# Recurrence of a gated delta rule: q/k/v projections from fp32 to three fp32r passes, turns in another order

## What is computed

```python
q = einsum('btd,cd->bct', h, Wq)      # k and v likewise; h is (4, 1024, 256), C = 1024
q = silu(causal_conv(q))              # depthwise, four taps, bias; k and v likewise
k = k / norm(k)
a, b = sigmoid(h Wa + ba), sigmoid(h Wb + bb)
S = clip(a*S + b*outer(v - a*(S k), k), -5, 5)     # per token, batch and head
y = S q
y = y * silu(h Wg + bg);  out = y Wo
```

## Time and profile before

| | us |
|---|---|
| runs of the kernel | 1858.39, 1866.88, 1870.13 |
| median | 1866.88 |
| span of the profiled execution | 1869.6 |
| that execution's own time | not listed apart; the nearest listed run is 0.5 above the span |
| front, to the first `turn_matrix` | 0 to 55.5 |
| turns (first to last `clear_x`) | 57.5 to 1109.6 |
| last chain, with gate products | 1170 to 1247 |
| `attn_out` | 1247 to 1510 |
| `moe` | 1510 to 1870 |

### The profile page before, as it was taken

How to read it: one execution, slowest core, us unless ns; L and a number is a source line. 1 busy time by engine, 2 the same in 40 slices (tenths; PEclk the granted TensorE clock), 3 DMA queues, 4 the chain that set the end, 5 groups by cost and what they waited for, 6 DMA issues and landing times. The chain is left out here.

```text
span 1869.6 us, 59680 instructions
## 1 busy us (share of the span) xinstructions
PE 1620.9 (87%) x24736; PEld 1142.6 (61%) x24736; DVE 1389.8 (74%) x1892; ACT 895.2 (48%) x1768; POOL 1127.0 (60%) x1362
## 2 busy tenths in 40 slices
PE   7778999999988989999988988835999848999997
PEld 4445666666666656566656666625888836666664
DVE  8777888888898888898898887447787664444443
ACT  5745555555655655655556555313444232222221
POOL 0657768768767767768777768017343103666664
PEclk9989989989999999989999988977999859999998
DMA  5221231231231231231231230246333163455543
GB/s 184 49 53 25 69 91 37 67 93 37 67 92 37 67 93 36 67 93 36 69 92 36 65 75 26 69 144 227 135 128 110 46 230 79 94 93 100 96 91 51
DMA packets 89465, 156.59 MB, mean 84 GB/s; under 512 B 15708, under 2 KB 54116, under 8 KB 88108
## 3 DMA queue, kind: packets, MB, share of 16 engines
q1 hardware_dynamic: 73292, 124.80, 22.6%
q0 software_dynamic: 15904, 27.93, 8.1%
HBM read 112.56 MB, written 40.12 MB: 82 GB/s over the span
## 5 line engine op out<-in xcount | busy, mean ns | idle before, releaser
L1386 PE MATMUL d_ps<-hT,turn_shared 128*128 128x512 f32 x768 | 402.8, 632 | 8.4 <-DVE d_Vp L1171 4.6
L953 POOL TENSOR_TENSOR turn_shared<-turn_shared,d_tmp 128x31 f32<-128x31 f32 (+15 forms) x496 | 289.7, 584 | 38.9
L948 POOL TENSOR_TENSOR d_tmp<-turn_shared 128x31 f32<-128x31 f32 (+15 forms) x496 | 286.4, 577 | 38.9
L1024 DVE SCALAR_TENSOR_TENSOR turn_shared<-d_ps,d_cw,turn_shared 128x1023 f32<-128x1023 f32 (+2 forms) x192 | 245.3, 1278 | 15.0 <-ACT turn_shared L682 12.6
L742 ACT ACTIVATE d_S<-d_S,gamma_chunk 128x64 f32<-128x64 f32 x448 | 130.9, 340 | 184.5 <-DVE d_S L1052 144.6
L2539 POOL DMA_INDIRECT m_xt<-rows_scratch,m_slot_i x71 | 70.2, 989 | 183.3 <-DVE m_slot_i L2632 95.7
L1386 PEld LDWEIGHTS d_ps<-hT,turn_shared 128*128 128x128 f32 x768 | 126.8, 192 | 87.6 <-issue 71.4
L2526 ACT ACTIVATE m_hm<-m_ps,m_b_tile 128x128 f32<-128x128 f32 x284 | 80.9, 368 | 206.3 <-PE m_ps L2706 206.3
L122 PE MATMUL o_po<-wo_split,y_high 128*128 128x256 f32 x512 | 101.7, 302 | 44.8 <-DVE y_low L115 44.8
L2549 POOL DMA_INDIRECT out<-m_yo,m_slot_i x71 | 114.2, 1608 | 41.2 <-issue 20.3
L2696 PE MATMUL m_ps<-m_w,m_xs 128*128 x284 | 136.2, 602 | 1.6 <-DVE m_xs L2641 1.0
(11 more groups left out here) (251 smaller groups left out, 3737.2 us busy)
## 6 DMA issues: line engine op xcount, KB each, us to landing
turn_shared<-steps_scratch SPq DMA_DIRECT2D x64, 256.0 KB, 4.2
d_qg<-gamma_scratch SPq DMA_DIRECT2D x64, 256.0 KB, 5.0
y_scratch<-d_yT SPq DMA_DIRECT2D x256, 64.0 KB, 1.8
d_arow<-ab_scratch SPq DMA_DIRECT2D x128, 128.0 KB, 3.1
y<-y_scratch SPq DMA_DIRECT2D x8, 2048.0 KB, 8.7
m_w<-w_in SPq DMA_DIRECT2D x16, 512.0 KB, 10.0
turn_shared<-x_by_half_in SPq DMA_DIRECT2D x8, 512.0 KB, 6.8
rows_scratch<-gates SPq DMA_DIRECT2D x4, 1024.0 KB, 11.6
```

Source lines behind the costliest of these rows:

```text
L948: nc.gpsimd.tensor_tensor(tv, Tq[:, s + 1:, s].rearrange("p (r a) -> p r a", a=1).broadcast_to([P, left, known]), X[:, s, 0:known].rearran ...
L953: nc.gpsimd.tensor_tensor(X[:, s + 1:, 0:known], X[:, s + 1:, 0:known], tv, ALU.subtract).then_inc(s_sub, 1)
L1024: nc.vector.scalar_tensor_tensor(out=dst[:, j + 1:], in0=src[:, 0:T - 1 - j], scalar=cw[:, u // BP % 2, n, 2 - j:3 - j], in1=dst[:, j + 1: ...
L1386: return nc.tensor.matmul(dst[:, g, :], w[:, m % 2, n, dc, :], hT[:, dc, at:at + G], start=(dc == 0), stop=(dc == DC - 1))
```

## The change

It does four things.

1. **Projections.** `proj` calls `three`: each of the 24 products of a turn becomes three fp32r passes over high and low parts of the weights and of the input. The parts of the input are made in the front: ACT writes the high part (`high_part`, one 128x1024 instruction for each of the eight pieces), POOL the low part (`low_part`, a subtraction of 128x1024). The parts of the weights are made for every turn and each of q, k, v: ACT `high_weights` and POOL `low_weights`, 128x256 each. The low part takes the place of the raw weights, and there is one buffer, so a load must wait for the projections of the turn before.
2. **Order of turns.** u now runs over the blocks first: turns 0 to 7 are batches 0 and 1, turns 8 to 15 batches 2 and 3.
3. **One pair on chip.** High and low parts of two batches take the room of `hT`. The parts of batches 2 and 3 go to DRAM from a staging buffer in the front (`store_input`), those of batches 0 and 1 after it (`store_pair`, 4 MB). Turn 7 loads batches 2 and 3 (`load_pair`, 2 MB each), turn 15 batch 0 again for the gate; `load_gate_input` and `load_h` fetch the parts for the other gate products.
4. **Splits of the input leave DVE**: `split_input` and `split_h` are gone, and the gate reads its moving operand in pieces of 32 tokens out of the stored parts.

The core of the diff (SP, ACT and POOL issue orders shortened to the new calls with their neighbours; the order on PE is the same, and on DVE only the splits go):

```diff
+    def high_part(act, g):
+        act.wait_ge(s_e, g + 1)
+        if g >= GH * BP + 2:
+            act.wait_ge(s_hst[g % 2], 32 * ((g - GH * BP) // 2))
+        nc.scalar.activation(part_of(0, g).bitcast(F32R), h_full[:, g % 2], ACT.Identity).then_inc(s_hh, 1)
+    def low_part(pool, g):
+        pool.wait_ge(s_hh, g + 1)
...
+        nc.gpsimd.tensor_tensor(part_of(1, g).bitcast(F32R), h_full[:, g % 2], part_of(0, g),
+                                ALU.subtract).then_inc(s_hl, 1)
+    def store_input(sp, g):
+        sp.wait_ge(s_hl, g + 1)
+        for a in range(2):
+            sp.dma_start(h_d[a, :, :, g * G:(g + 1) * G], h_sp[:, g % 2, a]).then_inc(s_hst[g % 2], 16)
     def alphas(act):
         act.wait_ge(s_a, B * GH)
+        for k in range(2):
+            act.wait_ge(s_hst[k], 16 * GH * BP)
@@ SP @@
-            def weights(m): ...
+            def weights(u, n):
+                if u and n == 1:
+                    sp.wait_ge(s_kproj, 2 * u)
+                elif u:
+                    sp.wait_ge(s_qproj, 4 * u - 2 + n)
+                sp.dma_start(w_raw[:, n], wqkv[block_of(u)][:, n]).then_inc(s_w[n], 16)
             step_rows(0, 0)
+            f.store_input(sp, 4)
             step_rows(0, 1)
+            f.store_input(sp, 5)
+            weights(1, 1)
+            f.store_input(sp, 6)
+            f.store_input(sp, 7)
...
             f.store_alphas(sp)
+            weights(1, 2)
             step_rows(1, 1)
             step_rows(2, 0)
+            store_pair()
             for it in range(1, TURNS + 2):
+                if new_k:
+                    weights(un, 1)
+                    conv_weights(un)
                 if prep:
                     gamma_rows(u)
                 if bound:
                     store_y(tb, 1)
+                if new_k:
+                    weights(un, 0)
+                if it in (M - 1, TURNS - 1):
+                    load_pair(it, 0, BP if it == M - 1 else 0)
+                if it == M - 1:
+                    load_pair(it, 1, BP + 1)
+                if new_k:
+                    weights(un, 2)
@@ ACT, front @@
             f.keep(act, 0)
+            f.high_part(act, 0)
             f.root(act, 1)
             f.keep(act, 1)
+            f.high_part(act, 1)
             f.logits(act, 0)
+            high_weights(0, 1)
...
+            f.keep(act, 4)
+            f.high_part(act, 4)
             first_k(0, 0)
-            f.keep(act, 4)
+            f.logits(act, 4)
             f.keep(act, 5)
+            f.high_part(act, 5)
+            high_weights(0, 0)
+            f.logits(act, 5)
             f.keep(act, 6)
+            f.high_part(act, 6)
             first_k(0, 1)
+            f.logits(act, 6)
             f.keep(act, 7)
+            f.high_part(act, 7)
             silu_k(0, 0)
...
             first_v(0, 1)
             f.alphas(act)
+            high_weights(1, 2)
             silu_v(0, 1)
             first_k(1, 0)
@@ ACT, loop: high_weights(un, 1) in slot 0, (un, 0) in slot 4, (un, 2) in slot 9 @@
@@ POOL, loop @@
                 if prep:
                     clear_x(u)
-                    solve(u)
+                    solve(u, range(8))
+                if new_k:
+                    low_weights(un, 1)
+                if prep:
+                    solve(u, range(8, CH - 1))
...
                     decay_k(u, 1)
+                if new_k:
+                    low_weights(un, 0)
+                    low_weights(un, 2)
@@ PE @@
             def proj(dst, n, b2, u, i):
-                m, g, dc = u // BP, i // DC, i % DC
-                at = (2 * (u % BP) + b2) * T + g * G
-                return nc.tensor.matmul(dst[:, g, :], w[:, m % 2, n, dc, :], hT[:, dc, at:at + G],
-                                        start=(dc == 0), stop=(dc == DC - 1))
+                g, dc = i // DC, i % DC
+                at = b2 * T + g * G
+                return three(nc, dst[:, g, :], lambda a: w_sp[a][:, n, dc, :], lambda a: h_in[:, a, dc, at:at + G],
+                             dc == 0, dc == DC - 1)
```

More of the change, by code:

```diff
@@ L452, with __init__, __call__, first @@
 AT_KT, AT_VT, AT_Z = (0, 0), (1, 1), (1, 1)
+class Early:
+    def __init__(self, nc, stack):
+        self.nc, self.stack = nc, stack
+    def __call__(self, name, *shape):
+        return self.stack.enter_context(self.nc.sbuf_tensor(name, list(shape), F32))
+    def first(self, name, *shape):
+        with ExitStack() as for_now:
+            return for_now.enter_context(self.nc.sbuf_tensor(name, list(shape), F32))
 def delta_fast(nc, sem, x, cT, wmod, rw, ident_d, ones2_d, wab, bab, tri_d, ident, ones2, modT, rw_sb, gates_s, s_loaded,
[L456 removed]
+               wqkv, convp, mask_d, h_in, h_d, w_raw, w_sp, btT, gtok, dec, gC, ab_s, a0_s, g_s, y_s, fmax, flag, wg, bg, turn,
+               gate1, held, split, bg_sb, s_gate):
     s_gw, s_hi, s_ws, s_hs, s_gp, s_g = s_gate
[L458 removed]
+    s_c, s_ar = sem("d_const"), sem("d_alpha_rows")
+    s_w = [sem(f"d_weights_{n}") for n in "qkv"]
+    s_wh, s_wl = [sem(f"d_weights_high_{n}") for n in "qkv"], [sem(f"d_weights_low_{n}") for n in "qkv"]
+    s_cw = [sem("d_conv_even"), sem("d_conv_odd")]
+    s_pair, s_pst = [sem(f"d_h_pair_{b2}") for b2 in range(2)], sem("d_h_stored")
     s_kproj, s_kfirst, s_ksilu = sem("d_k_proj"), sem("d_k_first"), sem("d_k_silu")
@@ L635, in _ @@
             f.load(sp, 0)
-            weights(0)
+            conv_weights(0)
+            for n in (1, 0, 2):
+                weights(0, n)
             f.load(sp, 1)
@@ L670, in _ @@
                     alpha_rows(tc, 0)
-                if prep and u % BP == BP - 1 and u // BP + 2 < M:
-                    weights(u // BP + 2)
                 if it == TURNS - 1:
@@ L841, in _ @@
             first_q(0, 1)
+            high_weights(1, 1)
             first_v(0, 0)
@@ L873, in _ @@
                         keep_w(tc, 1)
+                    if new_k and c == 0:
+                        high_weights(un, 1)
                     if prep and c == 1:
@@ L892, in _ @@
                         carry_state(tc, 5)
+                    if new_k and c == 4:
+                        high_weights(un, 0)
                     if prep and c == 5:
@@ L909, in _ @@
                         carry_state(tc, 10)
+                    if new_k and c == 9:
+                        high_weights(un, 2)
                     if new_k and c == 10:
@@ L953, in substitute, with low_weights, solve @@
                 nc.gpsimd.tensor_tensor(X[:, s + 1:, 0:known], X[:, s + 1:, 0:known], tv, ALU.subtract).then_inc(s_sub, 1)
-            def solve(u):
-                scale_rows(u)
-                for row in range(CH - 1):
+            def low_weights(u, n):
+                pool.wait_ge(s_wh[n], u + 1)
+                nc.gpsimd.tensor_tensor(w_sp[1][:, n].bitcast(F32R), w_raw[:, n], w_sp[0][:, n],
+                                        ALU.subtract).then_inc(s_wl[n], 1)
+            def solve(u, rows):
+                for row in rows:
+                    if row == 0:
+                        scale_rows(u)
                     substitute(u, row)
@@ L993, in decay_k @@
                                         ALU.mult).then_inc(s_kd, 1)
+            for g in range(2):
+                f.low_part(pool, g)
+            low_weights(0, 1)
+            for g in range(2, 6):
+                f.low_part(pool, g)
+            low_weights(0, 0)
+            for g in range(6, B * GH):
+                f.low_part(pool, g)
+            low_weights(0, 2)
             clear_x(0)
-            solve(0)
+            solve(0, range(10))
+            low_weights(1, 1)
+            solve(0, range(10, CH - 1))
+            low_weights(1, 0)
             gamma_k(0)
@@ L999, in _ @@
             decay_k(0, 1)
+            low_weights(1, 2)
             for it in range(1, TURNS + 2):
@@ L1985, in _ @@
             nc.vector.memset(raw[:, 0:4], 0.0).then_inc(s_z, 1)
+            dve.wait_ge(s_h, 32)
+            for dc in range(DC):
+                nc.vector.tensor_tensor(hT[:, dc, :], hT[:, dc, :], h_low[:, dc, :], ALU.add).then_inc(s_hj, 1)
             with dve.Fori(0, M) as m:
@@ L2216, in load_x, with load_h @@
                 sp.dma_start(held(g), x[:, g * GT:(g + 1) * GT, :]).then_inc(s_loaded[g % XHOLD], 16)
+            def load_h(b):
+                for a in range(2):
+                    sp.dma_start(h_s[b % 2][:, a], h_d[a, :, :, b * T:(b + 1) * T]).then_inc(s_hs, 16)
             load_y(0)
```

246 lines of the change are left out of this document (147 added, 99 removed).

## The result

The changed kernel takes 1893.2 us (median of 4 runs, 1887.8 to 1900.1), the kernel before 1867.9 in the same session: a ratio of 1.0143, 95% interval 1.0111 to 1.0175. That is slower by more than the 1% that a measurement tells, and 1.2 us above the range of 1856 to 1892. The profiled execution took 1896.0, its span is 1894.4; against the profiled 1869.6 it is 24.8 us longer, and that is the sum to be explained.

The account below looks back on a forecast made before the run. The prediction took a turn's loop, with POOL's triangular solution setting its floor, as the bound. Terms 8.0 - 1.3 + 4.5 + 0.5 - 4 - 2.2 - 1.0 = +4.5 us gave 1871 us, range 1856 to 1892.

Parts of the forecast that it names:

- So POOL sets a floor ..., and the whole excess over it is 1.4 us: Turns 1 to 14: POOL's solution and the shortest tail give 68.7 us under a turn of 70.06.
- Heads: 14 x 0: From `clear_x` to `rows_of_x` in fourteen turns: cheaper products and added POOL work leave the mean at 45.6; no change.
- Products: Projections on PE: three fp32r passes take 0.96 us for 1.12, saving 3.8 us of PE a turn.
- Rival 4: Projections: passes cost as much as fp32, savings vanish and heads grow; +20 us, 1887; chance 0.04.
- POOL in the head: `low_weights(un, 1)` after row 7 of `solve` adds 0.73 us, raising the head's floor to 45.6.
- Tails: From `rows_of_x` to the next `clear_x`: cheaper products save 0.3 us a turn, -4 over fourteen.
- Front: Start to first `turn_matrix`: ACT's added splits and a store wait move it from 55.5 to 63.5, +8.0 (+3 to +13).
- The wait of `high_part(7)`: In the front, ACT waits for `store_input(5)` to land, starting at 52 where it could at 50.3; +1.7 us.
- The wait behind `alphas`: Turn 0: `high_weights(1, 2)` waits 4.8 us for its weights, delaying `first_k(1, 0)`; +4.5 us, bounds 3 and 6.
- Stores and loads of the pair: 4 MB of stores ahead of turn 2's weights: +0.5 us, bounds 0 and 8; turn 7's 2 MB loads: nothing.
- Last preparation and chain: Turn 15 and behind: shorter q and v products give -2.2 us, the split at the end -1.0.
- Rival 1: Tails grow because idle PE runs longer at half clock; mean tail 25.2, +19.5 us, 1886; chance 0.20.

Follow-up runs that it names:

- The fixed position: Kernel before, with tiny PE products (30 in turn 1, 11 in later turns) so each turn fills 11 blocks of 256 instructions; 1857.7 us (0.9942).
- the 48 products: Changed kernel plus 48 products of 32x32 (191 PE instructions) in PE's idle time ahead of piece 6; 1872.0 us (1.0024).
- The mended front: Changed kernel with 46 small products, `high_weights(1, 2)` behind `first_k(1, 1)`, and two POOL subtractions waiting for DVE's normalisations; 1867.2 us (0.9980).
- control: Changed kernel plus 64 small products (255 PE instructions, a block less one) ahead of piece 6; 1896.3 us (1.0156).
- that edit alone: Changed kernel with `high_weights(1, 2)` moved on ACT from behind `alphas` to behind `first_k(1, 1)`; 1898.5 us (1.0162).
- the low parts cleared: Changed kernel with each of the eight POOL subtractions of 128x1024 replaced by a POOL memset of the same tile; 1885.5 us (1.0102).
- shifted by 192 with waits: Changed kernel with 192 more PE instructions (384 waits already over) before its first real one; 1885.7 us (1.0090).
- at its bad position: Kernel before with tiny PE products, 48 in turn 1 and 11 in later turns, starting turns about 127 to 140 instructions into a block; 1901.0 us (1.0192).

## Why the prediction was wrong

**The step that failed is the account of the turns: "So POOL sets a floor ..., and the whole excess over it is 1.4 us", with the term "Heads: 14 x 0".** The sum had -3.5 us for turns 1 to 14 (tails -4, stores +0.5, heads nothing); they took 7.0 more, with heads of 46.5 on the mean instead of 45.6. The floor was right, and no head ended before POOL's solution. But what lifts turns above the floor I put down to "PE and DVE were the late ones" and never asked why they were late. The rows of the kernel before had the answer. Its six heads of 45.9 or more (turns 1, 4, 7, 9, 10, 13) have each one stall of PE on "issue", 0.8 to 1.5 us long, and the other eight have none. Turn 4, from 341.28:

```profile
345.81 0.34 PE L1633 MATMUL d_ps<-d_U,d_ktok 64*64 64x64 f32 x7 [1.52 <-issue]
```

The fixed position takes the heads of turns 2 to 14 to 44.9 and the stalls go. I counted what the added instructions cost to execute and not that they move the code. At the bad positions this costs the changed kernel 22 us in fourteen turns (987.8 against 965.4 and 964.6), and it is nearly the whole of 1893.2 minus 1871: with another position the same kernel takes 1872.0. That this comes near the forecast's 1871 is in part luck, since two terms below are too small and the kernel before has stalls of its own, 11 us of them (1868.9 against 1857.7). At good positions of both the change costs 14.3 us (1872.0 and 1857.7; 10.7 between the profiled executions), not 4.5.

**Products: right.** PE was busy 897.3 us in turns 1 to 14. It is 859.1 in the changed kernel, and 845.3 with the 48 products, without most of the stalls: 52.0 / 14 = 3.7 a turn, forecast 3.8. Rival 4 is out.

**POOL in the head: the mechanism right, the size smaller.** `low_weights` takes 0.74 there, but the floor rose by 0.4 (44.9 to 45.3), not 0.7. L1355 was to start within 0.3 us of POOL's last row in nearly all turns; it does in turns 2 to 5 and in no other of 1 to 14, but in twelve of the fourteen in the run with 48 products (all but 7 and 14).

**Tails: right in sign, a little larger.** 23.3 where 23.8 was the floor, forecast 0.3 less. Mean 24.0.

**Front: mis-sized, +14.0 for +8.0 and outside the upper bound of 13.** I let POOL's subtractions run "beside" ACT and asked only what they cost POOL. They held DVE's normalisations (6.43 and 5.14 for 2.7), at least 3.1 us at the first `turn_matrix`. That is the price I had weighed for the solution and not for the front: the GPSIMD Engine Reference of the Trainium skill (section Specifications) says that GpSimd contends with DVE instructions with two SBUF inputs or in a 2-port performance mode. L350 has one tensor and two per-partition scalars in SBUF; that section does not say whether it is one of these, and the rows say that it is held up. The rest, some 3 us, goes with ACT waiting 8.46 us for PE: PE turned piece 6 late, and at 1.2 GHz after standing idle for 4.96. The mended front takes that away and brings `first_k(0, 1)` to 48.7, but then loses as much to the store and to another slow stretch of PE, so what this part is worth by itself stays open. The wait of `high_part(7)`, forecast at 1.7, fell due only there.

```profile
52.03 0.68 ACT L297 ACTIVATE ab_logit<-d_ps,bab_sb 32x512 f32<-32x512 f32 x1 [8.46 <-PE d_ps L431]
...
55.03 1.19 ACT L800 ACTIVATE turn_shared<-d_ps,d_cw 128x1024 f32<-128x1024 f32 x1
```

`first_k(0, 1)` starts at 55.0 in the changed kernel, for a forecast of 47.0, and `first_k(0, 0)` at 38.7 for 35.1.

**The wait behind `alphas`: right,** 4.27 for 4.8, and worth 4.6 in the head of turn 0 for 4.5 (below). What the head of turn 0 lost beyond it is PE's clock. In the first 7 us of turn 0 the granted clock is 0.51 in the changed kernel and 1.00 with the 48 products ahead of piece 6 (columns as in the windows above), and the first projections of q are ready 5 us later:

```profile
71.50:78.50 7.00, 7.00 (x64) 6.07 (x63) 1.57 (x4) 1.28 (x2) 5.64 (x11) 0.51 0.12 40
```

```profile
72.00:79.00 7.00, 6.28 (x27) 3.71 (x26) 6.78 (x10) 6.63 (x8) 5.64 (x11) 1.00 0.19 63
```

The heads of turn 0 make a square: slow start and wait 55.9 (changed kernel, control), slow start without the wait 51.2 and 51.3 (that edit alone, mended front), quick start with the wait 50.9 to 51.2 (five runs), quick start without it 46.4; before the change it was 46.1. Each is worth 4.6 to 4.9.

The slow start goes with a stall of the same kind as those in the turns. In the changed kernel PE stands 1.19 us on "issue" just ahead of turn 0, goes on 1.5 us after a 16 KB load has landed, and from 68.2 on its clock is at 1.2 GHz for 10.2 us:

```profile
68.26 0.80 PE L141 MATMUL d_ps<-h_pair,w_high 128*128 128x512 f32 x1 [1.19 <-issue]
```

The control and the run with no wait behind `alphas` have the stall there too (1.27 and 0.91), and the five quick starts with the wait and the one without it have none. (The mended front has its slow start behind the 5.01 us of idle PE.) The run with the low parts cleared has the same code positions as the changed kernel and no stall there, so the position alone does not decide it, and I could not have foreseen which start a kernel gets.

**Stores and loads of the pair.** 4 MB behind the front: nothing to be seen, forecast 0.5 (8 MB cost turn 1 11 us, 79.4 for 68.4). The loads in turn 7 were costed at nothing. In every run of the changed kernel, wherever its code stands, PE has a stall on "issue" of 0.9 to 1.8 us at about 27 us into that turn, while the second 2 MB are on their way (341 to 407 GB/s) and 1.3 to 1.6 us behind a load of its program. That the 2 MB cause it was not tested. It goes with 1.3 us in the run with 48 products (69.9 for 68.6), and 2.8 in the one shifted by 192 with waits.

**Last preparation and chain: right in sum,** 3.2 less as forecast (43.7 for 45.2 in the head, 1.6 less behind it). That the figures meet is partly luck: the head of turn 15 lies anywhere from 42.8 to 47.0 in the runs of the changed kernel, and this stretch takes 756.5 to 759.2 in them, 760.0 to 761.9 in those of the kernel before.

**Rival 1** (tails grow at half clock) had the right means, a granted clock that falls when PE stands idle between groups, and a total nearer the measured one, 1886, but the wrong place and cause: mean tail 24.0, far from its 25.2, and the half clock stands behind the stalls in the heads (0.77 in the window shown). Of my own tests of failure one spoke: the first `clear_x` of turn 1 came 21 us later, outside 8 to 14. The other two, heads under 45.3 and tails over 25, did not, and neither would have caught heads that grow.

## What to carry to other kernels

Where PE's program is unrolled, look at its waits on "issue" and at the count of its instructions per turn, modulo 256, before blaming or praising a change of a per cent. Time a kernel at two or three positions of its code, shifted by small products in PE's idle time, and compare kernels at their best. When work goes to POOL beside DVE, price it on DVE, by what DVE runs at that time, as well as on POOL.

## What the runs showed of the hardware

PE's program comes in loads of 16 KB, 256 instructions. In twelve traces of 202 to 206 loads no two of them start less than 3.2 us apart, and stalls of over 1 us in the heads end 1.2 to 1.6 us after a landing. The fastest 256 instructions of PE in the changed kernel's trace start within 1.1 us. My reading, not tested by itself, is that a burst of small products that uses up a block faster than the loads come runs dry. Here such a stall of 1 to 4 us on a chain makes a turn of 68.6 us longer by 1 to 6. In the changed kernel each of the eight stalls in the heads of turns 6 and 8 to 14 is followed by 3.4 us at 1.2 GHz (6.8 in turn 6); in the kernel before at its bad position only two of eleven are (turns 4 and 14), so the half clock is an addition and not the stall's price itself. Runtime: NRT & Kernel Launch in the Trainium skill (section Instruction fetch mechanics) gives the same blocks of 256 instructions, but says that the fetch is hidden and the cost of crossing a border mostly so. The measurement decides: 43 us of 1858 hung on it in the kernel before. What sets the 3.2 us, and why heads keep to the floor at positions of about 5 to 95 and 180 to 205, was not tried. (In the kernel before, the turns at 187 to 203 have slow tails, of 24.9 to 27.2.)

Eight DVE normalisations of 128x256 (`tensor_scalar`) took 2.67 us alone, 6.43 beside two POOL subtractions of 128x1024 in SBUF, and 3.4 beside POOL memsets. DVE's statistics (eight of 128x256, from 28.34 to 30.99) were not held up, 2.65 us with a POOL subtraction beside them from 29.91 on. A wait that is already over costs PE some 40 ns, an estimate: 15.5 us for 384.
